# The denominators' place in the third tile of a linear-attention kernel

## The reference

```python
qp, kp, v = phi(x @ Wq.T + bq), phi(x @ Wk.T + bk), x @ Wv.T + bv   # phi = elu + 1
kv   = kv + kt (outer) vt          # state, per head 32 x 32, over time
ksum = ksum + kt
num  = qt @ kv
den  = qt . ksum + 1e-6            # one number per head and token: the denominator
out  = num / den                   # then out @ Wo.T + bo, and the residual
```

## Time and profile before

| what | us |
|---|---|
| median of three runs | 1915.71 (1914.94 to 1915.79) |
| the profiled execution | 1916.06 |
| its span in the trace | 1914.3 |
| PE busy | 1890.7 (99% of the span) |
| PEld busy | 1659.6 (87%) |
| DVE busy | 1569.2 (82%) |
| POOL busy | 889.8 (46%) |
| ACT busy | 663.8 (35%) |

### The profile page before, as it was taken

How to read it: one execution, slowest core, us unless ns; L and a number is a source line. 1 busy time by engine, 2 the same in 40 slices (tenths; PEclk the granted TensorE clock), 3 DMA queues, 4 the chain that set the end, 5 groups by cost and what they waited for, 6 DMA issues and landing times.

```text
span 1914.3 us, 60181 instructions
## 1 busy us (share of the span) xinstructions
PE 1890.7 (99%) x25412; PEld 1659.6 (87%) x25412; DVE 1569.2 (82%) x3356; ACT 663.8 (35%) x1298; POOL 889.8 (46%) x981
## 2 busy tenths in 40 slices
PE   7999999999999999999999999999999999999997
PEld 6888888888888888888888888888888888888887
DVE  7888787888879888778878888887888897888888
ACT  4333333323333332333333433333333333323331
POOL 4345554455443554534554445544345553455422
PEclk9999999999999999999999999999999999999999
DMA  6343234333243432343323334333443234333222
GB/s 215 101 128 112 96 106 128 118 118 112 90 127 119 127 121 74 123 125 116 123 89 118 117 112 136 100 98 113 128 128 112 85 114 130 117 117 113 89 73 90
DMA packets 171197, 217.97 MB, mean 114 GB/s; under 512 B 24368, under 2 KB 85808, under 8 KB 170928
## 3 DMA queue, kind: packets, MB, share of 16 engines
q1 hardware_dynamic: 170928, 214.13, 35.4%
HBM read 151.02 MB, written 63.04 MB: 112 GB/s over the span
## 4 chain that ended last, share of the span: by engine, by line
PE 95%; DVE 2%; POOL 1%; DMA 1%; issue 0%; SPq 0%; ACT 0%; POOLq 0%; DVEq 0%
PE ring L684 38%; PE ring L666 36%; PE ring L758 7%; PE num_ps L788 6%; PE num_ps L771 3%; PE num_ps L801 2%; PE ring L730 1%; PE ring L743 1%; DMA v_tok<-in_wv_t 1%; DVE s_mask L973 0%; PE ring L654 0%; DVE stats L1091 0%; DVE den L1220 0%; DVE res L1084 0%; DVE o_lo L1215 0%
## 5 line engine op out<-in xcount | busy, mean ns | idle before, releaser
L1315 POOL TENSOR_TENSOR k_sum<-k_sum,q_raw 128x512 f32<-128x512 f32 x128 | 165.3, 1291 | 545.0 <-DVE q_raw L984 545.0
L883 ACT ACTIVATE e_tmp<-ring,bias_n 128x512 f32<-128x512 f32 x256 | 175.9, 687 | 509.3 <-PE ring L666 508.7
L973 DVE TENSOR_TENSOR s_mask<-ring,causal 128x512 f32<-128x512 f32 x512 | 315.0, 677 | 0.0
L684 PE MATMUL ring<-wv_hi,xt_hi 128*128 128x260 f32 x1024 | 298.9, 292 | 0.0
L684 PE MATMUL ring<-wv_hi,xt_lo 128*128 128x260 f32 x1024 | 289.2, 282 | 0.0
L684 PE MATMUL ring<-wv_lo,xt_hi 128*128 128x260 f32 x1024 | 289.2, 282 | 0.0
L684 PE MATMUL ring<-wo_hi,o_hi 128*128 128x260 f32 x1016 | 284.8, 281 | 1.3 <-ACT o_hi L938 1.3
L684 PE MATMUL ring<-wo_lo,o_hi 128*128 128x260 f32 x1016 | 285.7, 282 | 0.0
L684 PE MATMUL ring<-wo_hi,o_lo 128*128 128x260 f32 x1016 | 285.5, 284 | 0.2 <-DVE o_lo L1215 0.2
L938 ACT ACTIVATE o_hi<-num_ps 128x512 fp32r<-128x512 f32 x127 | 75.8, 597 | 465.9 <-PE num_ps L788 465.9
L666 PE MATMUL ring<-xt_hi,wk_hi 128*128 128x512 f32 x512 | 207.2, 405 | 3.4 <-DVE xt_lo L1042 1.7
(11 more groups left out here) (147 smaller groups left out, 3955.4 us busy)
## 6 DMA issues: line engine op xcount, KB each, us to landing
x_tok<-in_x SPq DMA_DIRECT2D x128, 256.0 KB, 3.8
res<-in_x SPq DMA_DIRECT2D x128, 256.0 KB, 2.8
out<-res SPq DMA_DIRECT2D x128, 256.0 KB, 2.1
x_in<-in_x_t SPq DMA_DIRECT2D x124, 256.0 KB, 4.7
keys_turned<-k_turned SPq DMA_DIRECT2D x112, 256.0 KB, 2.0
k_tok<-keys_turned SPq DMA_DIRECT2D x448, 64.0 KB, 2.1
x_rows<-moments_rows SPq DMA_DIRECT2D x31, 512.0 KB, 3.6
k_t<-in_wk_t SPq DMA_DIRECT2D x4, 256.0 KB, 4.5
```

Of the source, the lines that this page charges most:

```text
L684: mm = pe.matmul(bank[:, 0:HW], rows[a](k), w[b][:, k, h, :], start=n == 0, stop=n == 3 * KD - 1)
L883: act.activation(e_tmp[:, m], bank, ACT.Relu, bias=bias_n[:, m, g:g + 1], scale=-1.0).then_inc(phi_relu.handle, 1)
L973: dve.tensor_tensor(s_mask[:, j], ring[:, st.bank(u)].rearrange("p (g t) -> p g t", g=KD), repeat(causal, KD), ALU.mult).then_inc(free[st. ...
L1315: pool.tensor_tensor(k_sum[:, g], k_sum[:, g], q_raw[:, g], ALU.mult).then_inc(prod.handle, 1)
```

## The change

On PE, in the steps with both attention and projections, the denominators of tile 2 are issued after the state's update and before the values product; before, they were issued after the values product and before the scores. In the first step, which has projections only, their place stays. On ACT the copy `den` is issued ahead of `o_hi` instead of behind it. DVE, POOL and SP keep their order.

```diff
                     from_state(st, c)
                     add_state(st, c)
+                    if c == 2 and proj:
+                        denominators(st)
                     from_tile(st, c)
                 if c == 1 and not attn:
                     sum_gates(pe, (0, 1))
                 if c == 2 and not attn:
                     sum_columns(pe)
-                if c == 2 and proj:
                     denominators(st)
                 if not last and attn:
                     scores(st, st.off, c + 1)
...
                 if c == 1 and st.alone():
                     exponential(act, 4)
+                if c == 2 and proj:
+                    u = ("DEN", 0)
+                    act.wait_ge(full[st.bank(u)].handle, st.filled(u))
+                    for m in part_begun(st.off - 1):
+                        act.wait_ge(chosen.handle, (m + 1) * CHOOSE_STEPS)
+                    act.activation(den, ring[:, st.bank(u), 0:BT // 2], ACT.Copy,
+                                   bias=DEN_EPS).then_inc(free[st.bank(u)].handle, 1)
...
                 elif attn:
                     act.wait_ge(summed.handle, summed.at(st.lin(TPB, st.off, c + 1)))
                     act.activation(o_wide[0], num, ACT.Copy).then_inc(o_hi.handle, 1)
-                if c == 2 and proj:
-                    u = ("DEN", 0)
-                    act.wait_ge(full[st.bank(u)].handle, st.filled(u))
-                    for m in part_begun(st.off - 1):
-                        act.wait_ge(chosen.handle, (m + 1) * CHOOSE_STEPS)
-                    act.activation(den, ring[:, st.bank(u), 0:BT // 2], ACT.Copy,
-                                   bias=DEN_EPS).then_inc(free[st.bank(u)].handle, 1)
                 if attn:
                     keep_state(st, c)
```

## The result

The changed kernel takes 1942.49 us (median of four runs, 1939.15 to 1942.87) against 1915.75 for the kernel before (1914.94 to 1916.4) on the same chip: ratio 1.0136, 95% interval 1.0118 to 1.0154. It is slower, as forecast, by 26.7 us where 19.0 were forecast, and the time lies 1.5 above the range of 1926 to 1941. The profiled execution was the fastest of the four, 1939.15 with a span of 1937.4 against 1914.3, so what the trace can account for is 23.1 us.

What follows compares the result with a forecast made beforehand. PE, busy 1890.7 of 1914.3 us, was taken to bound the kernel. rden's longer wait adds 24 x 0.79 = 19.0, other terms 0: 1916.06 + 19.0 = 1935.1, median 0.35 lower, 1934.7; range 1926 to 1941.

Steps and rivals of the forecast that it cites:

- PE's own sum: PE's matmul time per block: denominators take 0.87 to 0.88 in the new place, so change 0, at best -0.01.
- The wait for POOL's product: Denominators on PE need POOL's fourth product; at the tightest 1.73 us to spare, so cost 0.
- ACT: Copy den, 0.38 long, ends at 919.61 before o_hi is wanted at 920.08, so cost 0.
- DVE's chain 0.87 later: Values product ends 0.87 us later, and so does everything behind it in DVE's order, up to rden.
- The room of 0.96: DVE's chain from o_hi had 0.96 us to spare before PE's spread reciprocals (R); the change takes 0.87.
- rden waits to the end of POOL's instruction and 0.28 more: On DVE, rden started under a POOL normalisation waits it out and ends 0.28 us after it.
- the five blocks that stay free: Four blocks near 631, 866, 1101 and 1571 us, and the last without POOL normalisation: no added time.
- s + 0.53: rden's added wait, s running from its old start to POOL's next instruction: 0.89 us on average in 24 blocks.
- The shift alone: Rival: rden keeps its present waits and only shifts; +5.7 us, 1921.4; chance 0.08.
- POOL's gaps: Rival: later rden falls between POOL instructions, not slower; 0 to -0.9 us, 1914.8; chance 0.06.
- Rival three: Longer wait: POOL's phase drifts or a second wait follows; with the longest wait everywhere +40 us, 1956; chance 0.06.
- The second wait at the outputs' bank: Outputs' first bank, freed by the first mask about 923.80 for a PE matmul at 924.06; 0.26 suffices, cost 0.

Runs made afterwards that it cites:

- the two later profiles: Traces of the unchanged changed kernel, run twice more: spans 1938.1 and 1934.2 us, series medians 1939.54 and 1936.74 us.
- the third profile: Trace of the changed kernel, unchanged, in its last repeat with more rounds: span 1934.2 us, series median 1936.74 us.
- the experiments with POOL's start: Changed kernel with POOL's normalisations held until denominators' bank filled, den copied or values product done: 1961.39, 1971.90, 1985.73 us.
- the second and third experiments: Kernel before with an extra DVE reciprocal of 128x128: 1937.13 us; kernel before with half the denominators ahead of the values product: 1926.99 us.
- one further step of 0.41: Changed kernel, POOL's second normalising instruction held until rden is written, plus a 128x64 DVE reciprocal: 1932.90 us, against 1920.14 without that reciprocal.

## Why the prediction was right in kind and too small

- **PE's own sum, costed at 0 to -0.01: wrong by 0.04 per block, 1.3 us.** In blocks without a gap the period is 58.31 where it was 58.27. The denominators take 0.87 as said, but the values product behind them takes 1.08 to the scores (930.65 to 931.73) where it takes 1.03 in the fourth tile.
- **The wait for POOL's product, 0: right.** PE shows no gap there.
- **ACT, 0: right.** den ends at 931.35, o_hi starts at 931.84; undoing the move changed nothing.
- **DVE's chain 0.87 later: right, 0.91 measured** (from the state's update to rden; 0.04 more by the slower values product). The room of 0.96 held too; the dummy work on DVE showed the loss at a shift smaller than it.
- **rden waits to the end of POOL's instruction and 0.28 more: right**, in 26 blocks, 24 + 2 as counted; so was R 0.95 behind it, and the five blocks that stay free. (In the two later profiles one of these five has a gap too.)
- **The size of that wait, s + 0.53: too small. This is the step that failed.** The prediction took s from one trace, with normalisations that "start from a DMA of the tile before and don't move", and allowed a drift of 0.1. Over the 26 blocks the forecast comes to (19.0 + 0.87) / 26 = 0.76 of gap, measured 0.88: 3.1 us. The sixth POOL instruction starts at 7.29 instead of 7.18 and is 0.03 longer than the 1.59 put down. The DMA is issued at the same point of the tile (4.58 before the update in both), but lands 0.11 later on average in this execution, and POOL starts 0.13 later. It is this execution's phase and not the change's doing: in the third profile of the same kernel, at 7.19, these 26 blocks give 20.1 us, and with ACT's copy back, at 7.18, 19.9, which is the forecast's 19.9. There the block near 880 adds 1.1 and 1.2.
- **Sum.** 19.0 + 3.1 + 1.3 = 23.4 against 23.1 in the profiled execution. That one's 1939.15 lies in the range; the median of its series, 3.3 higher, does not.
- **What is open.** The other three runs of the first series lie 3.2 to 3.7 above the profiled one, and no trace covers them. By 26 blocks that would be a phase another 0.13 later (an estimate), which the experiments with POOL's start make likely and nothing shows. Two later series have medians 3.0 and 5.8 lower, both within 1926 to 1941, so the changed kernel varies between series by more than the 2.2 + 2.4 = 4.6 either way of the likeliest case; the three profiles tie 1.7 us of it to POOL's phase.
- **Rivals.** The shift alone (1921.4) is refuted by the second and third experiments; POOL's gaps (not slower) occur in five blocks, as counted. Rival three's drift of POOL's phase did occur, 0.11 of it, and not its 40 us. The second wait at the outputs' bank exists: it was costed at 0 with 0.26 of cover where 0.14 does, and one further step of 0.41 made R 0.39 late by it. No version tried beats the kernel before.

## What to carry to other kernels

Moving a step past another on the bounding engine can leave that engine's sum almost alone and still cost 1.4%, because every engine that waits for the step that was passed gets later against the next deadline; count the room to that deadline with the longest duration that the late instruction shows, not the shortest. Where two engines lock each other out, the cost is a matter of phase: read which instruction of the other engine will be under way at the new time, and take its spread between blocks and between runs as the error of the forecast. Work added or held back on an engine with time to spare is a good probe for this, but look up first which other instructions of the kind that gets locked out it will then fall on: POOL held back by 2.3 spared rden and cost 40 us at `xt_lo`.

## What the runs showed of the hardware

- rden (two operands in SBUF, 0.475 alone) started under a POOL instruction ends 0.28 to 0.29 after it, from one kernel to the next and however much of that instruction is left above 0.2; `xt_lo` (the same kind, 128x512, 0.69 alone) ends 0.54 to 0.56 after it. So it is a wait and not a slower pace.
- Who starts first goes first, at each instruction anew. In all traces rden takes 0.48 when it starts 0.045 or more ahead of a POOL normalisation, which then takes up to 1.95 instead of 1.6; at 0.03 ahead or less (the longest one before, 1.893, starts 0.02 ahead) it waits for the whole of it.
- DVE instructions that read PSUM and the reciprocal hardly change under POOL: in the changed kernel the reciprocal takes 1.74 with and without, the masks 0.63 to 0.69 in both cases, o_lo 0.65 to 0.69.
- The values product, 32 records of 128x32 tiles with 128 columns, took 1.03 from its start to that of the 32x128 scores in the fourth tile and 1.08 behind matmuls of the same tile shape with 256 columns. Why was not tried.
- The moments' DMA (`x_rows`, 512 KB) landed 3.3 to 3.9 us after its issue in the trace of the kernel before, with the issue at about the same point of each block, and the first instruction that uses it started 3.4 to 4.2 us after the issue.
